# A graph layer, attention and experts in one kernel: each engine's order of work in a step put anew

## What is computed

```python
xn = layernorm(x)                                   # x: 6250 nodes x 256
# 1. graph attention over 100,000 edges (src, dst)
Wh = xn @ W_w + W_b
e  = leaky(Wh[dst] @ a1 + Wh[src] @ a2 + a_b)       # one score an edge
att = softmax of e over the edges with the same src
g  = relu(segment_sum(att * Wh[dst], src))
# 2. linear attention, 8 heads of 32
q, k = elu(xn @ Wq.T) + 1, elu(xn @ Wk.T) + 1
m  = (q @ (k.T @ v)) / (q . sum(k)) @ Wproj.T + bproj
x  = x + g + m
# 3. eight experts, two taken by each node
t  = layernorm(x)
comb = routing weights of the two best experts, 0 elsewhere     # 6250 x 8
x  = x + t + sum over e of comb[:, e] * (gelu(t @ w1[e] + b1[e]) @ w2[e] + b2[e])
```

## Time and profile before

| | |
|---|---|
| median of 3 runs | 2280.97 us (2277.75 to 2284.66) |
| the profiled execution's own time | 2273.09 us |
| its span | 2271.3 us |
| PE busy | 1741.7 us, 77% |
| DVE busy | 1675.5 us, 74% |
| ACT busy | 961.7 us, 42% |
| POOL busy | 997.4 us, 44% |
| mean granted TensorE clock | 0.888 |

### The profile page before, as it was taken

One profiled execution on the slowest core, in us unless ns is written; L12 is line 12 of the kernel. 1 busy time (PEld: TensorE's weight loads), 2 busy tenths in 40 slices (PEclk: granted clock), 3 DMA queues, 4 the chain that ended last, 5 costly groups with the idle time before them and its releaser, 6 DMA issues.

```text
span 2271.3 us, 40228 instructions
## 1 busy us (share of the span) xinstructions
PE 1741.7 (77%) x13588; PEld 1269.5 (56%) x13588; DVE 1675.5 (74%) x4215; ACT 961.7 (42%) x2288; POOL 997.4 (44%) x996
## 2 busy tenths in 40 slices
PE   4788887561788567778875787778887888889998
PEld 2456564350667356656653555555555555566666
DVE  5888888671566667676767788888888888885665
ACT  5331222130333222222223566656666565666554
POOL 3000001615466666555666566666566666610000
PEclk9997887695899778887986899999899999999999
DMA  5011111112455444333333333333333334830000
GB/s 169 6 66 44 56 50 44 28 62 81 135 156 156 129 117 118 99 95 95 99 87 91 81 88 92 85 92 91 83 92 85 93 82 90 80 39 10 11 20 12
DMA packets 121716, 182.21 MB, mean 80 GB/s; under 512 B 21614, under 2 KB 92158, under 8 KB 121470
## 3 DMA queue, kind: packets, MB, share of 16 engines
q0 software_dynamic: 45568, 120.06, 22.7%
q1 hardware_dynamic: 75904, 59.25, 8.4%
HBM read 152.43 MB, written 26.63 MB: 79 GB/s over the span
## 4 chain that ended last, share of the span: by engine, by line
DVE 37%; PE 32%; issue 17%; ACT 5%; another core or an unknown queue 4%; DVEq 2%; POOL 1%; DMA 1%; ACTq 0%; SPq 0%; POOLq 0%
PE bank L1210 5%; PE bank L1226 4%; DVE big L1471 3%; DVE work L1751 3%; DVE big L1476 3%; PE bank L941 3%; DVE work L1532 2%; DVE work L1549 2%; DVE mloc L1554 2%; DVE scr L1576 2%; DVE big L1473 2%; DVE big L1478 2%; PE bank L1087 2%; PE bank L1096 2%
## 5 line engine op out<-in xcount | busy, mean ns | idle before, releaser
L641 POOL DMA_INDIRECT work<-table,tiles x904 | 918.6, 1016 | 560.3 <-PE bank L1078 299.0
L1226 PE MATMUL bank<-big 128*128 128x256 f16 x2352 | 317.9, 279 | 0.0
L1076 PE MATMUL bank<-work,scr 128*128 128x257 f16 x904 | 269.8, 298 | 33.4 <-DVE scr L1576 22.9
L1210 PE MATMUL bank<-scr,big 128*128 128x512 f16 (+1 forms) x1248 | 282.0, 376 | 2.9 <-ACT big L849 2.9
L1077 PE MATMUL bank<-work,scr 128*128 128x256 f16 x904 | 271.6, 300 | 4.6 <-issue 4.5
L1078 PE MATMUL bank<-work,scr 128*128 128x257 f16 x904 | 270.4, 299 | 4.9 <-issue 4.7
L1226 PEld LDWEIGHTS bank<-big 128*128 128x128 f16 x2352 | 235.6, 100 | 35.5
L1044 PE MATMUL bank<-identh,work 128*128 128x128 f16 x904 | 81.6, 243 | 209.9 <-DVE work L1549 176.8
L1576 DVE SCALAR_TENSOR_TENSOR scr<-scr,gg,bank 128x257 f32<-128x257 f32 x452 | 217.7, 482 | 33.0 <-issue 15.5
L967 PE MATMUL bank<-big 128*128 128x208 f16 x1568 | 173.8, 265 | 71.5 <-DVE big L1478 65.6
L967 PEld LDWEIGHTS bank<-big 128*128 128x128 f16 x1568 | 149.3, 101 | 96.9 <-issue 92.1
(11 more groups left out here) (340 smaller groups left out, 3462.7 us busy)
## 6 DMA issues: line engine op xcount, KB each, us to landing
work<-table,tiles POOLq DMA_INDIRECT x904
scr<-normed_cols SPq DMA_DIRECT2D x98, 128.0 KB
table<-big SPq DMA_DIRECT2D x49, 129.0 KB, 2.1
normed_rows<-scr SPq DMA_DIRECT2D x49, 128.5 KB, 2.8
big<-normed_rows SPq DMA_DIRECT2D x49, 128.5 KB
normed_cols<-big SPq DMA_DIRECT2D x49, 128.0 KB, 1.7
xs<-in_x_dram SPq DMA_DIRECT2D x4, 1536.0 KB, 15.2
out_dram<-work SPq DMA_DIRECT2D x48, 128.0 KB
```

Of the source, the lines that this page charges most:

```text
L641: pool.indirect_dma_start(G[:, r, j, :], None, table, bass.IndirectOffsetOnAxis(ap=col[:, t:t + 1], axis=0)).then_inc(rows_in[r // GS], 16)
L1076: pe.matmul(of[:, 0:D + 1], hi, Gh[:, r, j, 0:D + 1], start=(j == 0), stop=False)
L1210: mm = pe.matmul(bank[5 + f][:, 0:n * P], w1p[pw][:, e, h, f * P:(f + 1) * P], x2p[b % 2][px][:, h, 0:n * P], start=(h + m == 0), stop=(h ...
L1226: mm = pe.matmul(of, hTp[ph][:, k % 2, f, (j + c) * P:(j + c + 1) * P], w2p[pw][:, e, f, :], start=False, stop=(f == 1 and m == 2))
```

## The change

It has five parts.

1. **Rank products by node tile.** HB is read tile outer, column inner (ten neighbours of two bytes, then a jump of 400 bytes), `vrow` is laid out the same way, and the reduction reads its PSUM bank with a stride of ten words. The bases are worked out with the tiles on the partitions, which puts two small operations more in `bases`; two transfers in place of four fill `vrow`.
2. **Order within a step.** See the diff: on PE `spread` stands before the second half of `down` and before the second pair of keys, `expanded` moves a step later and to the front, `queries` stands before `projected`. On DVE `mixed` and `divided` come a step later and early; `queries_one` and `keys_one` come after `shifts`; the second half of `add` comes after `shifts`; `split` moves from the front half of step s+1 to the end of step s. On ACT the cast leaves `hidden` (it is now `hidden_hi`) and stands behind OT and the exponential's table load.
3. **Waits.** `up` waits for the Gelu before it and no longer for the cast (`m_g` in place of `m_hi`).
4. **The second bias.** The product of ones by b2 in each `down` goes. In its place: `combine` writes the routing weights as f16 parts (three small operations more), PE turns them (four transposes a batch), ACT copies them, PE multiplies them by the eight rows of b2 (one product a node tile), and DVE adds the result (`add_bias`, two operations a batch). The preparation of b2 (L1814 to L1817 before, on one partition) becomes one of 72 partitions by 256.
5. **Schedule.** A_FROM = CTX_AT + 4 in place of + 5, so F_AT begins at step 50 and the tail has one step less.

```diff
-        A_FROM = CTX_AT + 5
+        A_FROM = CTX_AT + 4
...
-                    pe.matmul(bank[k % 2][:, 0:n * W], ranks[:, :], HB[b % 2][:, :, c:c + n].rearrange("p w c -> p c w"),
+                    pe.matmul(bank[k % 2][:, 0:n * W], ranks[:, :], HB[b % 2][:, :, c:c + n],
                               start=True, stop=False)
-                    pe.matmul(bank[k % 2][:, 0:n * W], lift[:, :], vrow[:, c * W:(c + n) * W],
+                    pe.matmul(bank[k % 2][:, 0:n * W], lift[:, :],
+                              vrow[:, 0:(z - a) * W].rearrange("p (w c) -> p w c", w=W)[:, :, c:c + n],
...
                     last = dve.tensor_reduce(srank[:, c:c + n],
-                                             bank[k % 2][:, 0:n * W].rearrange("p (c w) -> p c w", w=W), AX.X, ALU.max)
+                                             bank[k % 2][:, 0:n * W].rearrange("p (w c) -> p c w", w=W), AX.X, ALU.max)
...
-                for half in range(2):
-                    for k, of in enumerate((vh, vl)):
-                        pool.dma_start(
-                            vrow[k:k + 1, half * n * W:(half + 1) * n * W].rearrange("a (c w) -> a c w", w=W),
-                            of[0:n, half * W:(half + 1) * W]).then_inc(s_row[b % 2], 16)
+                for k, of in enumerate((vh, vl)):
+                    pool.dma_start(vrow[k:k + 1, 0:2 * n * W].rearrange("a (w c) -> a w c", w=W),
+                                   of[:, 0:2 * n]).then_inc(s_row[b % 2], 16)
...
 # ACT, one step
-                if s - 2 in A_AT:
-                    reciprocals_sb(A_AT[s - 2])
...
                 if s + 2 < NS:
                     one_hot_turned(s + 2)
                     if s in UP_AT:
                         act.activation(ready[:, s:s + 1], epsc[:, :], ACT.Exp)
+                if s - 2 in FIRST:
+                    combine_turned(FIRST[s - 2])
+                if s in UP_AT:
+                    hidden_hi(*UP_AT[s])
+                if s - 2 in A_AT:
+                    reciprocals_sb(A_AT[s - 2])
...
 # PE: waits of up, the bias
                 if k:
-                    pe.wait_ge(m_hi, k)
+                    pe.wait_ge(m_g, 2 * k)
...
-                    pe.matmul(of, onesq[:, :], b2p[:, e * D:(e + 1) * D], start=True, stop=False)
...
+            def combine_turns(b, u):
+                pe.wait_ge(m_cp, b + 1)
+                pe.wait_ge(e_s3, scored(u))
+                for j in range(of_batch[b]):
+                    mm = pe.transpose(bank[2][0:KB, 256:512].bitcast(F16)[:, j * P:(j + 1) * P], cparts[:, j, :],
+                                      identh[:, :])
+                mm.then_inc(m_ct, 1)
+
+            def bias(b, h, u):
+                pe.wait_ge(m_cT, b + 1)
+                pe.wait_ge(e_s3, scored(u))
+                if BIAS0[b] + h:
+                    pe.wait_ge(m_badd, BIAS0[b] + h)
+                j, n = halves(b)[h]
+                for c in range(n):
+                    mm = pe.matmul(bank[2][:, c * D:(c + 1) * D], combT[:, (j + c) * P:(j + c + 1) * P], b2s,
+                                   start=True, stop=True)
+                mm.then_inc(m_bias, 1)
...
 # PE, one step
+                for p in K_AT.get(s, ())[0:1]:
+                    keys(p)
+                if s - 3 in A_AT:
+                    expanded(A_AT[s - 3])
...
-                for p in K_AT.get(s, ()):
+                if s in DOWN_AT:
+                    down(*DOWN_AT[s], 0)
+                if s + 2 < NS:
+                    spread(s + 2)
+                if s in DOWN_AT and len(halves(DOWN_AT[s][0])) > 1:
+                    down(*DOWN_AT[s], 1)
+                for p in K_AT.get(s, ())[1:]:
                     keys(p)
...
+                if s in A_AT:
+                    queries(A_AT[s])
                 if s - 3 in A_AT:
                     projected(A_AT[s - 3])
-                if s in A_AT:
-                    queries(A_AT[s])
-                if s - 2 in A_AT:
-                    expanded(A_AT[s - 2])
-                if s in DOWN_AT:
-                    for h in range(len(halves(DOWN_AT[s][0]))):
-                        down(*DOWN_AT[s], h)
-                if s + 2 < NS:
-                    spread(s + 2)
...
 # DVE, one step
-                for p in K_AT.get(s - 1, ()):
-                    keys_one(p)
-                if s - 1 in A_AT:
-                    queries_one(A_AT[s - 1])
-                if s - 2 in A_AT:
-                    reciprocals(A_AT[s - 2])
-                if s in DOWN_AT:
-                    split(*DOWN_AT[s])
+                if s - 4 in A_AT:
+                    mixed(A_AT[s - 4])
+                if s - 3 in A_AT:
+                    divided(A_AT[s - 3])
                 if s in ADD_AT:
-                    for h in range(len(halves(ADD_AT[s][0]))):
-                        add(*ADD_AT[s], h)
+                    add(*ADD_AT[s], 0)
...
+                for h in range(2):
+                    if s - 3 - h in FIRST and len(halves(FIRST[s - 3 - h])) > h:
+                        add_bias(FIRST[s - 3 - h], h)
                 if s + 2 < NS:
                     shifts(s + 2)
+                if s in ADD_AT and len(halves(ADD_AT[s][0])) > 1:
+                    add(*ADD_AT[s], 1)
+                for p in K_AT.get(s - 1, ()):
+                    keys_one(p)
+                if s - 2 in A_AT:
+                    reciprocals(A_AT[s - 2])
+                if s - 1 in A_AT:
+                    queries_one(A_AT[s - 1])
...
-                if s - 3 in A_AT:
-                    mixed(A_AT[s - 3])
-                if s - 2 in A_AT:
-                    divided(A_AT[s - 2])
-                if s in P_AT:
-                    weights_lo(P_AT[s])
+                if s in UP_AT:
+                    split(*UP_AT[s])
+                if s - 2 in P_AT:
+                    weights_lo(P_AT[s - 2])
```

138 lines of the change are left out of this document (91 added, 47 removed).

## The result

The changed kernel takes 2263.04 us (median of 6 runs, 2258.20 to 2272.17), the kernel before in the same comparison 2285.99: 0.990 of it, 95% interval 0.9885 to 0.9921. That is 23 us faster. Forecast were 2145 us and a range of 2070 to 2215: the sign was right, the size far off. The profiled execution took 2272.17 us, its span is 2270.4.

A forecast was written before the change was run, and what follows sets the result against it. It took each stage to have another limit: rings between PE and DVE in key and query steps, DVE nearest full in expert steps, PE in the tail. Terms 22 + 14 + 38 + 36 + 4 + 21 = 135 off 2281 gave 2146, named 2145, range 2070 to 2215.

The forecast's parts named there:

- Rank products: Sorting: near-contiguous reads make chunks cheaper, waits shrink; with vrow and bases 22 us off, bounds 45 off and 40 on.
- The strided reduction: Rival, sorting: L1436's strided PSUM read slows to about 2.75 us; 31 us on in all, 2312; chance 0.05.
- The tail: Tail: bias products gone (17), one step less (5.2), 3.5 on, `up` freed from the cast (2.5); 21 us off.
- The preparation of b2: Preparing b2: 256-element operations in place of 2048, 1.8 us against 5.8; 4 us off, at least 2.
- Key and query steps: Steps fall to 11.9 us from 13.1 (key, 14 off) and 13.4 (query, 38 off); bounds 0 to 25 and 68.
- its ring at `spread`: Key steps: DVE idles at L1521 until PE has done `spread`, last in PE's step; 50.7 us, 4.2 each.
- Again a ring: Query steps: DVE ends its step with `mixed` and `divided`, whose inputs PE makes late; waits of 28.3 and 17.6 us.
- Expert steps: Edge steps: 0.9 and 0.3 gained, 0.25 and 0.3 lost, 0.6 off a step; 36 us off, bounds 51 on, 72 off.
- The clock: Query steps: the clock, 0.83 in the profile, should be above 0.83 after the change.
- Steps stay held by what the profile can't name: Rival: steps can't go below about 12.3 us; 100 us off in all, 2181; chance 0.14.
- the next rival: Idling caused the unnamed waits; steps fall to POOL's pace, two 8 x 1.27 = 10.2; 212 off, 2070; chance 0.12.
- The cast comes too late: Rival, expert steps: `split` waits 0.85 us more a step, 15 on there; 84 off in all, 2197; chance 0.09.

The follow-up runs named there:

- old order: As a run: the changed kernel with each engine's turn in a step put back as before, new rank products and bias kept; 2251.30 us, 0.9854.
- e9: Changed kernel, full work, POOL issuing the second four gathers of a step only after that step's spread, on chip Z; 2085.45 us, 0.976.
- again: Second traces of the unchanged kernels, on one chip: the kernel before 2285.50 us, the changed kernel 2262.83 us.
- no gathers: Kernel before and changed kernel with the edge steps' row gathers left out after the first four steps; 2178.22 and 2122.48 us.
- e13: Changed kernel, unchanged, run again beside the kernel before on one chip; 2262.83 us, 0.9897.
- e15: New rank products and bias with the old order within steps, run again on the chip of e13; 2251.74 us, 0.9856.
- e11: New rank products and bias with the old order, gathers left out after four steps, on chip Z; 2116.83 us.
- e10: Like e9, with POOL's wait for spread, but the expert steps in their old order, on chip Z; 2102.01 us, 0.9829.
- chip Z: The chip on which e9, e10 and e11 ran; the kernel before took 2137.27 us there and not 2286.
- e3: Changed kernel with the cast of the hidden rows alone put back behind the Gelu; 2262.01 us, 0.9888.

## Why the prediction was wrong, by its own steps

**Rank products** were right: 22 off forecast (its own terms give 21.4, and its bound of 45 off is not worked out), 19 to 21 measured in sorting, 28 for the part by itself (interval 23 to 32). The run of ten is cheaper than the 0.45 us that I took: the next product starts 0.22 or 0.39 us later, by the clock's level. DVE sets the chunk, so this gained nothing more. The strided reduction costs nothing more, 0.66 us. The Trainium skill's page SBUF — State Buffer, section Door 1: The DMA port swizzle, has lines of 8 bytes in PSUM; for this read of DVE no run shows a cost of them.

**The tail** was forecast 21 off and came out 17.6 and 18.7 off. Its parts fit less well. The new bias alone brings some 7 (252 in the old order against 259), where 17 less 3.5 were forecast, and the order with the one step less brings 12, where 5.2 and 2.5 were. That the sum is near is partly luck. The preparation of b2 has its longest operations at 0.42 and 0.44 us instead of 2.28.

**Key and query steps** failed, and with them 52 of the 135 us. I forecast 11.9 us for both. Where no signal is held the new order takes 11.0 and 11.6 (e9, with all gathers), so the reading of PE's queue was even cautious. What failed is the other end: I took 13.1 and 13.4 as what the old order costs, and its ring at `spread` and the late inputs of `mixed` as the whole reason. Without gathers the old order takes 11.5 and 12.5. So 0.5 and 0.8 us a step were the change's. Holding and gathers cost the old order 1.3 to 1.4 us a step and the new one 1.6 to 2.1 (`again` against `no gathers`), so they eat the gain: on the same chip (e13 against e15) its key steps are equal and its query steps 0.46 longer than the old one's.

The step that failed is in the first section. At the key steps a wait of 4.2 us a step at the scores was put down to PE's order alone; without gathers 2.6 of it is left. At the query steps ("Again a ring") two waits, 28.3 and 17.6 us, were added up as one cause, though the larger was put down to "remote"; without gathers 2.2 us of 3.2 a step are left, so that ring was real, but a third of it was not the order's. And of what the new order did take away there, most came back at the maxima and `weights`, for which the sum had no term. A smaller slip lies in the step itself: 13.4 is 336 us over the 25 V's that start in them, while the V's of this trace stand 13.7 us apart from the 21st to the 45th.

**Expert steps**, 36 off forecast, are 21 to 28 on. The new bias was nearly as I put it: 0.25 us a step forecast, 0.23 to 0.33 found with its short waits (before to old order, on both chips), 14 to 19 us. The order was the miss: 0.9 gained at the scores and 0.3 in mid-step against 0.3 lost at `split`. Where nothing is held (e11, e9) the scores and `weights` gain 0.8 a step, `split` loses 0.4, the maxima and the additions 0.15 each: 0.08 a step in all, 5 us (0.2 a step by e10 and e9). Where signals are held the order costs 0.12 a step (e15 to e13), 7 us. The gain at the head was real and was given back further on, where DVE waits for the same PE and ACT.

**The clock** in the query steps was to rise above 0.83; it is 0.85, and 0.93 on chip Z.

**The rivals.** "Steps stay held by what the profile can't name" was the right one, at 0.14 and 2181 us. I let steps fall to 12.3 in it; it should have asked what sets the 12.3. Half of the answer was in the text of the next rival, 8 x 1.27 = 10.2 for the row of gathers; the landing behind it stood in no row. The Trainium skill's page Runtime: NRT & Kernel Launch, section Instruction fetch mechanics, with its fetch at a branch, does not explain these waits by itself: with the gathers gone the same branches are taken and DVE has none of the unnamed waits but the one at the first scores. "The cast comes too late" was there in small, 26 us of waits where nothing is held, and not what decided (e3). "The strided reduction" did not come.

**What stays open.** Why PE's signals are held when eight gathers run in a step and hardly when four do; whether the products themselves are held; and why one chip of four has none of it and takes 2137 us for the same program. There the sorting is 20 us shorter too, and the wait of 27.1 us at the first scores is missing. That single chip is shown by three kernels, all run at one time, with the kernel before timed beside them. The changed kernel itself did not run there, and the kernel before has no trace there; whether it is the chip or a state that it was in, no run shows. Nor did the old order run anywhere with all gathers and nothing held: the runs without gathers take away the gathers' load along with the holding.

On the other three chips no version with all the work beat both kernels clearly. The old order with the new ranks and bias is at 0.985 to 0.986 on two chips, against 0.990 for the change, 11 us, with intervals that overlap on the one chip where both ran side by side.

## What to carry to other kernels

A wait that the profile puts down to "remote", with the producer long done by its record, is a question to settle before an order is changed: take the times of the semaphore's increments, hold them against the ends of the producer, and look for what ends at the same moment. Price a new order by the step that it would have if nothing were late and the old order by the same measure; the difference of the two is its worth, not the new one against the measured old one. And when steps in which every engine has room keep a pace of their own (11.8 to 12.3 us here), look for the queue that runs through all of them, here POOL's gathers.

## What the runs showed of the hardware that was not expected

- Increments of `spread`'s semaphore by PE were recorded up to 6.6 us after the product's end in the changed kernel (7.6 with gathers of 64 rows) while POOL issued indirect transfers, in the stretch shown in a bunch 0.07 us apart. They were never over 0.02 us late without such transfers.
- In the changed order it goes by the number of gathers in a step, not by their size: 8 a step 363 to 375 us of lateness over the steps, with 128 or 64 rows each, 6 a step 174, 4 a step 49. With `spread` at the end of PE's step 8 a step make 123 to 149.
- It goes by the chip, or by the state that it was in: on three of four chips the kernel before took 2286 to 2291 us, on the fourth 2137. There the two traces with all gathers, at the same 1.26 us a gather, have no late signal.
- A moving operand with runs of ten f16 and then a jump of 400 bytes passed as fast as a contiguous one: the next product started 0.22 us after it at the upper level of the clock and 0.39 at the lower, for 490 columns; behind the contiguous L943 it was 0.38 at either. With a jump at every element it was 0.87 at either.
